# New merge tables for the two instruction streams of a one-core hybrid kernel

## The reference

```python
x = x + attn_a(layernorm(x))   # projection, softplus/exp/cos/sin, rotated scan over time, norm, projection
x = x + ffn(layernorm(x))
x = x + attn_b(layernorm(x))   # delta rule: S = S + beta k (v - k S), o = q S, layernorm
x = x + ffn(layernorm(x))      # the same weights

def ffn(x):
    h = silu(x @ w1.T * s1) * (x @ w2.T * s2)      # 256 -> 1024, twice
    h = gelu(h @ h1.T * sh1)                       # 1024 -> 1024
    h = gelu(h @ h2.T * sh2)                       # 1024 -> 1024
    return h @ w3.T * s3                           # 1024 -> 256
```

## Time and profile before

| | |
|---|---|
| Median of 3 runs | 2548.43 us (2544.89 to 2548.49) |
| The profiled execution, its own time | 2549.43 us |
| Its span | 2547.7 us |
| PE, PEld busy | 2259.9 us (89%), 2016.0 us (79%) |
| DVE, ACT, POOL busy | 1361.7, 1118.6, 843.0 us |
| Chain that ended last | PE 60%, DVE 22%, issue 8%, POOL 5% |
| First and last PE instruction of the stages, from the timeline | FIRST 147.1, PEEL 309.0, BODY 609.6 to 2107.3, LATE to 2295.6, LAST to 2446.6 |

### The profile page before, as it was taken

How to read it: one execution, slowest core, us unless ns; L and a number is a source line. 1 busy time by engine, 2 the same in 40 slices (tenths; PEclk the granted TensorE clock), 3 DMA queues, 4 the chain that set the end, 5 groups by cost and what they waited for, 6 DMA issues and landing times.

```text
span 2547.7 us, 61597 instructions
## 1 busy us (share of the span) xinstructions
PE 2259.9 (89%) x25057; PEld 2016.0 (79%) x25088; DVE 1361.7 (53%) x3348; ACT 1118.6 (44%) x2160; POOL 843.0 (33%) x1003
## 2 busy tenths in 40 slices
PE   4679988887999989999989988999899998898888
PEld 3558877776888878888888878888788887897888
DVE  4555374456735656466645657356663756546531
ACT  3347332452335733365334743357333663333323
POOL 3123332323333333332333333342333433233233
PEclk8779999997999999999999999999999999999999
DMA  7000000000010001000010000100010000000000
GB/s 252 1 1 1 1 18 18 1 1 3 24 28 2 1 19 30 7 1 2 18 33 4 1 3 18 35 2 1 7 32 17 1 2 18 24 5 18 17 11 9
DMA packets 85468, 43.84 MB, mean 17 GB/s; under 512 B 69936, under 2 KB 80048, under 8 KB 85168
## 3 DMA queue, kind: packets, MB, share of 16 engines
q1 hardware_dynamic: 81504, 28.11, 4.4%
q0 software_dynamic: 3664, 11.53, 1.4%
HBM read 27.05 MB, written 12.58 MB: 16 GB/s over the span
## 4 chain that ended last, share of the span: by engine, by line
PE 60%; DVE 22%; issue 8%; POOL 5%; DMA 2%; ACT 2%; DVEq 0%; SPq 0%; POOLq 0%; ACTq 0%
PE F L1279 27%; PE Q L1338 5%; PE F L1259 5%; DVE ti L1129 4%; DVE prod L1127 3%; PE F L1301 2%; PE Q L1395 2%; PE Q L1409 2%; PE Q L1372 2%; POOL hA_lo L588 2%; DVE hid L939 2%; PE Q L1436 2%; POOL rn L640 2%; PE Q L1504 2%; PE Q L1350 1%
## 5 line engine op out<-in xcount | busy, mean ns | idle before, releaser
L588 POOL TENSOR_TENSOR hA_lo<-hid,hA_hi 128x256 fp32r<-128x256 f32 (+1 forms) x384 | 358.4, 935 | 712.7 <-ACT hA_hi L717 406.4
L1279 PE MATMUL F<-hA_hi,h_sb 128*128 128x256 f32 x2048 | 506.9, 289 | 7.6 <-DVEq L942 4.8
L1279 PE MATMUL F<-hB_hi,h_sb 128*128 128x256 f32 x2048 | 501.2, 287 | 3.2 <-POOL hB_lo L588 3.2
L1279 PE MATMUL F<-hA_lo,h_sb 128*128 128x256 f32 x2048 | 489.9, 280 | 0.0
L1279 PE MATMUL F<-hB_lo,h_sb 128*128 128x256 f32 x2048 | 486.3, 279 | 0.0
L1279 PEld LDWEIGHTS F<-hA_hi,h_sb 128*128 128x128 f32 x2048 | 387.8, 189 | 19.3 <-DVEq L942 5.8
L1279 PEld LDWEIGHTS F<-hB_hi,h_sb 128*128 128x128 f32 x2048 | 384.9, 188 | 14.0 <-POOL hB_lo L588 5.4
L1279 PEld LDWEIGHTS F<-hA_lo,h_sb 128*128 128x128 f32 x2048 | 388.2, 190 | 1.7 <-issue 1.4
L1279 PEld LDWEIGHTS F<-hB_lo,h_sb 128*128 128x128 f32 x2048 | 386.3, 189 | 0.5 <-issue 0.5
L1259 PE MATMUL F<-xf_hi,w_sb 128*128 128x256 f32 x1024 | 277.2, 306 | 80.6 <-DVEq L942 57.0
L713 ACT ACTIVATE hid<-F,sh_sb 128x256 f32<-128x256 f32 x256 | 121.4, 474 | 397.6 <-PE F L1279 395.9
(11 more groups left out here) (196 smaller groups left out, 4124.6 us busy)
## 6 DMA issues: line engine op xcount, KB each, us to landing
h_sb<-h_dram POOLq DMA_DIRECT2D x2, 4096.0 KB, 23.8
x_sb<-x_dram SPq DMA_DIRECT2D x8, 512.0 KB, 4.3
a_scr<-amv SPq DMA_DIRECT2D x32, 128.0 KB, 2.3
au<-a_scr SPq DMA_DIRECT2D x8, 512.0 KB, 3.3
t_scr<-ti SPq DMA_DIRECT2D x8, 512.0 KB, 2.6
tbd<-t_scr SPq DMA_DIRECT2D x128, 32.0 KB, 1.9
out_dram<-x_sb SPq DMA_DIRECT2D x8, 512.0 KB, 3.0
w_sb<-w_dram POOLq DMA_DIRECT2D x3, 1024.0 KB, 8.3
```

What stands on the lines that cost most here:

```text
L588: pool.tensor_tensor(lo, hid[:, n % 2, 0:w, :], hi.bitcast(F32), ALU.subtract).then_inc(f_lo.handle, 1)
L1279: last = pe.matmul(ps[:, i * TOK:(i + 1) * TOK], w[:, k, o:o + P], part[:, k, :], start=(i == 0 and k == 0 and part is src[0]), stop=(i == ...
```

## The change

All 20 tables hold other numbers of the same length and sum; no instruction of PE, DVE, POOL or SP is added or taken away, only moved. Two lines of the diff:

```diff
 BODY_PLAN = {
-    "pe": ("2 1 2 0 0 0 2 0 0 1 0 1 0 1 1 1 30 1 1 1 1 0 1 0 0 1 1 1 0 0 1 1 1 1 0 2 0 2 0 0 2 1 1 2 0 1 1 "
-             "1 0 0 1 1 1 1 1 1 4 1 0 7 1 1 1 0 2 0 3 0 1 0 1 0 1 1 0 3 0 1 0 0 0 0 1 0 3 0 1 0 0 1 1 0 0"),
+    "pe": ("2 1 1 1 0 1 1 0 0 0 2 0 0 2 0 1 31 1 2 0 1 0 0 0 0 1 0 2 0 0 1 0 1 2 1 1 0 2 1 0 1 0 2 0 1 2 1 "
+             "1 0 0 1 0 1 1 1 1 5 1 0 7 1 0 2 0 2 0 4 0 1 0 1 0 0 1 0 3 0 1 0 0 0 0 1 0 3 0 0 0 0 1 2 0 0"),
```

## The result

| | before | after |
|---|---|---|
| Median of the runs | 2548.46 us (4 runs, 2544.89 to 2548.80) | 2574.56 us (4 runs, 2567.63 to 2579.93) |
| The profiled execution, its own time | 2549.43 us | 2567.63 us |
| Its span | 2547.7 us | 2565.9 us |

The ratio is 1.0099, with a 95% interval of 1.0086 to 1.0113: the change makes the kernel 1.0% slower, some 26 us. Forecast were 2541.8 us and a range that ended at 2560. So the two profiles differ by 18 us and not by 26.

The account below looks back on a forecast made before the run. TensorE's order bounds the kernel, through idle time and stream changes. Five iterations at -0.2 us give -1.0, the other stages -5.6: -6.6 from 2549.4 is 2542.8, median 1.0 lower, 2541.8 us; own range 2535 to 2548, whole range 2520 to 2560.

Parts of the forecast that it names:

- ssm_stage, +0.7: Body's ssm_stage: fewer visits and waits save time, ScalarE's second-chunk queue costs more; +0.7 us an iteration.
- The eight transposes of shT now stand inside that wait, -0.8: ssm_stage, after sT of the second chunk: transposes fill w1.5's 1.70 us wait for a product, saving 0.8 us an iteration.
- 2.0 us reach sout: ssm_stage: two Gelu pieces and loads ahead of copy yT on ScalarE delay sout, +2.0 us an iteration.
- Gated layer, -2.4: Body's second unit: 1.2 us gained at product 0, another 1.2 up to product 5; -2.4 us an iteration.
- Walk, +1.8: Body's walk: open half-steps and the third unit's gated pieces cost more than four fewer visits save; +1.8 us an iteration.
- PEEL, 0: PEEL: seven more open half-steps, +3.1 us, cancelled by xt's shorter wait, fewer visits and other gains; net 0.
- FIRST, -1.0: FIRST: a gain of 1.0 us, set between 0 and its 12.0 us of idle time.
- LATE, -2.7: LATE: w1.0's 2.09 us wait gone, one step and nine visits fewer, against more open half-steps; -2.7 us.
- LAST, -1.9: LAST: xt's 1.84 us wait for xnf gone, chunk chain -1.0, two more open half-steps +0.9; -1.9 us.
- C: Rival, slower: ScalarE's queue in ssm_stage costs 3.3 an iteration, gated gain lost at uw; 2560.3 us, chance 0.21.
- My B: Rival, nothing net: half-step costs replace what 46 fewer visits save, VectorE's gain only makes up; 2548.4 us, chance 0.18.
- The rule with 2.66 us for a switch on ScalarE: Trainium skill's rule adding a drain to each table load; two more loads cost 2.8 us more an iteration, giving 2555.6.

Follow-up runs that it names:

- body_ssm: The kernel before with the body's new tables from ssm_stage on alone: 15.6 us above before, ratio 1.0052.
- ssm_both: As body_ssm, with GpSimd's two xs products two low parts sooner and one Gelu piece behind the copy yT: 0.5 us below before, 0.9998.
- gated2: As body_gated, but with the pieces of TensorE, ScalarE and GpSimd at the inverse counted as before: 2.7 us above before, 1.0013.
- body_walk: The kernel before with the body's new tables for the walk alone, from uw to the first xn transpose: 10.3 us above before, 1.0036.
- rest_new: The kernel before with the new tables of FIRST, PEEL, LATE and LAST, the body's old ones kept: 7.9 us above before, 1.0030.
- best: The kernel before with xd_later's edit in the body and the new tables of LATE and LAST: 7.0 us below before, 0.9976.
- body_new: The kernel before with the four new tables of the body alone: 22.1 us above before, 1.0099.
- body_delta: The kernel before with the body's new tables up to the first xn transpose of ssm_stage, old ones behind it: 3.3 us above before, 1.0014.
- body_gated: The kernel before with the body's new tables up to the inverse (delta_stage chunks, second unit's gated layer): 5.8 us above before, 1.0019.
- yt_first: The changed kernel with one Gelu piece and its table load moved behind the copy yT of ssm_stage's first chunk, body only: 2571.81 us, ratio to before 1.0077.
- xd_sooner: The changed kernel with GpSimd's two xs products of ssm_stage's first chunk two low parts sooner, body only: 2563.88 us, ratio to before 1.0052.
- chg_both: The changed kernel with the edits of both yt_first and xd_sooner: 10.3 us above before, 1.0050.
- first_new: The kernel before with the new tables of FIRST alone: 4.9 us above before, 1.0021.
- peel_new: The kernel before with the new tables of PEEL alone: 3.9 us above before, 1.0015.
- xd_later: The kernel before with GpSimd's two xs products of ssm_stage's first chunk four low parts later, body only: 2.4 us below before, 0.9993.

## Why the prediction was wrong

*What bounds the kernel* was read rightly: it is TensorE's order and its waits. The terms of ssm_stage, of the gated layer and of the four other stages failed, and the range with them.

*ssm_stage, +0.7.* This is the step that cost most: measured +2.7 to +3.1 an iteration (body_ssm: 1.0052 of 2549, or the 15.6 us of the medians, by five). Two of its terms were wrong. "The eight transposes of shT now stand inside that wait, -0.8": they don't fill the wait, since they need `hat`, and `hat` is ready only half a us ahead of the product for which w1.5 waited (1111.27 by the timeline of VectorE, w1.5 starts at 1111.78). I saw who waits and not that both wait for the same chain of VectorE. And that chain became longer, as GpSimd's xdt and xD moved beside it; the wait grew to 2.8 us, and half clock followed. From the first xn transpose to the second projection, where I had -0.8, it is +0.2 without a dip and +1.8 with one (27.23 and 28.8 us for 27.02), and in the change a dip came in four of five iterations. "2.0 us reach sout": 1.05 did. The place and the cause were right (in the second chunk's ScalarE work, at the first chunk's sout) and the size was half. So the part that I had at nearly nothing was the larger part of the loss; with both places mended it is zero (ssm_both).

*Gated layer, -2.4.* w1.1 lost its 1.44 us and little came of it: 0.9 us up to uw in the trace, no gain in gated2. Both terms held as far as they go. Counted from the start of the first w3 piece on TensorE (974.19 before, 985.93 after), product 0 begins 1.2 us sooner and product 5 2.5. The step that failed is that I stopped counting at "up to product 5 two steps stand in place of three": the step that left stands between products 5 and 6 now, and product 6, for which the first hidden piece waits, is only 1.0 us sooner. VectorE before and after:

```profile
991.60 0.48 DVE L939 SCALAR_TENSOR_TENSOR hid<-F,s_sb,gate 128x256 f32<-128x256 f32 x1 [0.21 <-DVE ti L1129]
992.44 0.48 DVE L939 SCALAR_TENSOR_TENSOR hid<-F,s_sb,gate 128x256 f32<-128x256 f32 x1
...
1000.83 0.48 DVE L939 SCALAR_TENSOR_TENSOR hid<-F,s_sb,gate 128x256 f32<-128x256 f32 x1
1003.20 0.48 DVE L939 SCALAR_TENSOR_TENSOR hid<-F,s_sb,gate 128x256 f32<-128x256 f32 x1 [0.21 <-DVE ti L1129]
```

What sets the pace are pairs: two products and one substitution step take 3.26 us (994.09 to 997.35), two FFN pieces less, so each pair brings a wait of 1.1. By their third iterations, neither with a dip there, the waits of the gated layer sum to 5.4 us before and 4.8 after: the 1.44 are gone, and of the rest the most came back as a fourth wait of 1.1. The rival's reason, an inverse that is late, did not occur: uw has no wait for `tbd`.

*Walk, +1.8.* Right by the traces: +2.0 in that of the change, +1.6 in each iteration from uw to sT in that of body_walk. That body_walk is 10.3 us above before is in part clock. Its half-steps cost 0.3 to 0.4 us of waiting for `st` as forecast, in five of them; a sixth costs 1.26, since `st` is made behind a product that waits 1.28 us for a gate. I had 0.5 for that.

*PEEL, 0, and FIRST, -1.0.* Measured +3.9 and +4.9. In PEEL I costed the half-steps and the gain at xt and never asked what stands on VectorE between the walk and the first xn of ssm_stage; in FIRST I gave a gain without going through a single wait. Most of both is clock, though (0.9 and 1.1 at equal clock), which I had kept out. *LATE, -2.7, and LAST, -1.9*: the waits that I named went, 2.09 us at w1.0 and 1.84 at xt, but the open half-steps wait 0.45 us each in their place, and the waits of over 0.4 us sum to 12.0 us for 11.9 in LATE and 15.4 for 15.0 in LAST. At equal clock nothing of the forecast 4.6 us is found, neither in rest_new nor in best.

*Rivals.* The end on the slower side was the one that came, but by another mechanism than I had named (C: uw and `yT`), and 14 us beyond it. My B held the true sentence, that the half-steps eat what the visits save. The rule with 2.66 us for a switch on ScalarE didn't come true either: in the changed kernel, too, the function behind a load starts 1.30 us after it, and ten loads more cost ScalarE 13.7 us.

*The clock.* I had kept it out of the sum, as it was 0.99 in the body before; the page's rounding hides most of it. In the profiles the body has seven dips before and nine after (23.9 and 30.7 us at half clock), and each costs 1 us or so, 1.5 ahead of the second projection of ssm_stage. A least-squares fit over the first four iterations of all 17 traces (one length for each kernel, one price for the time at half clock) gives 0.28 us for each us at half clock, and clock-free lengths of 298.6 us before, 302.0 for the change, 297.8 for ssm_both, with 0.6 us left over. By that some 3.4 of the 4.1 us for an iteration are waits, the rest is clock.

The 241 timed executions whose granted clock is on record say the same for whole kernels: a fit with one time for each set of runs and one price gives 0.31 us (0.28 to 0.34) for each us at half clock, with the time at half clock taken as twice the missing share of the clock times the span. In us above before, by the medians and by this fit at equal time at half clock (each good to about 2):

| | medians | at equal clock |
|---|---|---|
| the change | 26.1 | 20.6 |
| body_new, rest_new | 22.1, 7.9 | 19.6, 1.8 |
| body_delta, body_ssm | 3.3, 15.6 | 9.2, 10.7 |
| body_gated, gated2, body_walk | 5.8, 2.7, 10.3 | 7.4, -0.4, 6.1 |
| yt_first, xd_sooner, chg_both | 23.0, 15.0, 10.3 | 14.4, 16.2, 8.0 |
| first_new, peel_new | 4.9, 3.9 | 1.1, 0.9 |
| xd_later, best, ssm_both | -2.4, -7.0, -0.5 | -6.4, -6.8, -1.4 |

(The runs of before beside the change list no clock; its row is taken against the mean of the four later sets.) At equal clock the parts add up where the medians don't: body_delta and body_ssm to 19.9 for body_new's 19.6. yt_first is 6 us below the change, as was expected of it, and xd_later 6 below before, as was expected too; best has no more than that. So the fits hold the clock still, but they don't say what an order does to it: the change has 197 us at half clock on average and before 183 to 186, and which wait of an order brings a dip isn't shown.

## What to carry to other kernels

When an order is changed, go through the tables of all engines at each place where a chain waits, the ones that seem idle too: here two products on GpSimd, 33% busy, cost the change some 11 of its 26 us, and most of that came through TensorE's clock. Before a step is costed as filling a wait, ask what that step itself waits for. Count the changes of stream last: 46 visits fewer at 0.20 us came with new waits of 1 to 6 us. And where the clock moves, compare iterations, or runs, with equal time at half clock.

## What the hardware showed that I had not expected

VectorE and GpSimd hold each other up when both work from SBUF. `seg` takes 1.21 us where it begins first and 2.06 where xdt began 0.1 us ahead of it; a rotation step 0.42 and 1.15; a low part on GpSimd 0.74 and 1.64 when VectorE's `seg` began ahead of it. The Trainium skill's SBUF — State Buffer, section Who interferes with whom, says that the two share one pair of ports as an exclusive lock, that a VectorE instruction with two SBUF inputs contends with a GpSimd instruction that reads SBUF, and that the order of issue decides which one is blocked. The traces agree: the slow rotation steps end 0.3 us behind GpSimd's instruction and the slow `seg` 1.1 us behind the end of xdt, not much less than its own 1.21, and which of the two engines is slow goes by the order of their starts. `xn`, which reads one tensor, is slow too, 1.13 us beside xD and 0.81 beside a low part for 0.4 elsewhere; that wasn't looked into.

TensorE falls to half clock for 3.4 us at a time, sometimes for several of these in a row. In the body of the changed kernel each of the nine dips begins within 1 us of the end of a wait of 1.2 to 2.8 us; but not each such wait has one (in yt_first the 2.81 us for `hat` has a dip behind it in three of five iterations), and in yt_first some dips begin with no wait over 0.2 us ahead. In xd_later w1.1 of the second unit waits 1.44 us in each iteration, and in the second no dip follows, in the third one does, 4 us later. The runs of the kernels with the new order of ssm_stage in the body also lie further apart: their standard deviations are 4.8 to 7.4 us, against 2.7 to 3.9 in the four later sets of before, and within a kernel the slower runs show less clock (0.960 for 0.964 in the change).
